# Linear attention of a decoder layer: part of the feature-map work moved from VectorE to GpSimd, and the key sums moved to the end of a tile

## What is computed

```python
def _feature_map(t, K):
    f = jnp.einsum('hdf,bhld->bhlf', K, t)
    feats = jnp.concatenate([jax.nn.softmax(f, axis=-1), jax.nn.softmax(-f, axis=-1)], axis=-1)
    return jnp.maximum(feats, EPS)
q = _heads(x @ Wq); k = _heads(x @ Wk); v = _heads(x @ Wv)
qf = _feature_map(q, Kq)
kf = _feature_map(k, Kk)
kv = jnp.cumsum(kf[:, :, :, None, :] * v[..., None], axis=2)
o = jnp.einsum('bhlf,bhldf->bhld', qf, kv)
z = jnp.einsum('bhlf,bhlf->bhl', qf, jnp.cumsum(kf, axis=2)) + EPS
```

## Time and profile before

| | |
|---|---|
| median of 3 runs | 1230.46 us (1229.52 to 1231.06) |
| the profiled execution | 1229.25 us, span in the trace 1227.0 us |
| mean granted TensorE clock | 0.982 |
| PE busy (share of the span) | 1117.3 us (91%) |
| DVE busy | 962.1 us (78%) |
| ACT busy | 611.1 us (50%) |
| POOL busy | 377.3 us (31%) |

### The profile page before, as it was taken

The page is one execution under the profiler, slowest core; times in us unless marked ns, Lnnn a source line. Parts: engine busy times, 40 slices in busy tenths (PEclk is TensorE's granted clock), DMA queues, the critical chain, the costliest instruction groups (busy, mean ns, idle before and its releaser), DMA issues. The chain is left out here.

```text
span 1227.0 us, 30062 instructions
## 1 busy us (share of the span) xinstructions
PE 1117.3 (91%) x11860; PEld 719.6 (59%) x11861; DVE 962.1 (78%) x1769; ACT 611.1 (50%) x1166; POOL 377.3 (31%) x355
## 2 busy tenths in 40 slices
PE   6698898899899999879999999999999957999996
PEld 5577777777788878643443344334444334666765
DVE  6889978987888788888788677877889556777757
ACT  4233343334333433227777677776788822444443
POOL 4432245222522222113201320222110414656651
PEclk9899999999999999999999999999999988999998
DMA  7100001000400000524720570065050144221225
GB/s 240 41 8 1 2 28 53 2 1 1 80 2 2 1 1 2 81 59 81 152 34 8 114 146 2 9 127 108 2 211 3 53 80 145 65 64 60 63 62 205
DMA packets 60045, 73.65 MB, mean 60 GB/s; under 512 B 14404, under 2 KB 51140, under 8 KB 59188
## 3 DMA queue, kind: packets, MB, share of 16 engines
q1 hardware_dynamic: 56132, 61.56, 21.0%
q0 software_dynamic: 3792, 10.36, 2.7%
HBM read 52.86 MB, written 18.78 MB: 58 GB/s over the span
## 5 line engine op out<-in xcount | busy, mean ns | idle before, releaser
L1791 DVE TENSOR_REDUCE neg_max<-pS 128x1 f32<-128x1024 f32 x238 | 284.9, 1220 | 56.2 <-PE pS L1574 56.0
L1706 ACT ACTIVATE pt<-pR 128x512 f32<-128x512 f32 x512 | 286.5, 600 | 80.1 <-PE pR L1597 75.3
L1597 PE MATMUL pR<-qs,ks 100*32 100x512 bf16 x2048 | 191.2, 383 | 3.1 <-ACT pt L1706 1.6
L1574 PE MATMUL pS<-ks,qs 100*32 100x512 bf16 x1904 | 145.9, 381 | 5.1 <-issue 1.9
L1611 PE MATMUL b_pO<-pt,b_v 128*32 128x512 f32 x1024 | 135.9, 605 | 2.9 <-ACT pt L1706 2.3
L1597 PEld LDWEIGHTS pR<-qs,ks 100*32 100x32 bf16 x2048 | 56.2, 96 | 95.3 <-issue 25.6
L324 POOL TENSOR_TENSOR kf<-kf,fsum 128x2048 f32<-128x2048 f32 (+1 forms) x17 | 58.2, 3422 | 163.8 <-DVE fsum L933 163.8
L324 POOL TENSOR_TENSOR qs<-qs,fsum 128x2048 f32<-128x2048 f32 (+1 forms) x17 | 58.5, 3446 | 142.7 <-DVE fsum L933 142.7
L1453 POOL COPY qs<-max_rows 3x512 bf16<-3x512 bf16 x60 | 36.6, 610 | 209.3 <-ACT max_rows L1699 206.3
L745 ACT COPY qfT<-pT 128x512 f32<-128x512 f32 x64 | 37.3, 582 | 122.7 <-PE pT L466 122.7
L1574 PEld LDWEIGHTS pS<-ks,qs 100*32 100x32 bf16 x1904 | 51.4, 97 | 74.3 <-issue 35.7
(11 more groups left out here) (376 smaller groups left out, 2270.8 us busy)
## 6 DMA issues: line engine op xcount, KB each, us to landing
qs<-q_scr SPq DMA_DIRECT2D x24, 256.0 KB
ks<-k_scr SPq DMA_DIRECT2D x7, 768.0 KB
k_scr<-f SPq DMA_DIRECT2D x18, 256.0 KB, 2.8
ks<-in_L_ffn_w_dram SPq DMA_DIRECT2D x2, 2048.0 KB, 11.1
ks<-in_L_ffn_w_dram SPq DMA_DIRECT2D x4, 1024.0 KB, 8.5
ks<-y_rows SPq DMA_DIRECT2D x16, 256.0 KB, 5.1
ks<-k_scr SPq DMA_DIRECT2D x6, 512.0 KB
cx<-in_ctx_dram SPq DMA_DIRECT2D x3, 768.0 KB, 12.3
```

Source lines behind the costliest of these rows:

```text
L1574: ins = pe.matmul(pS1[q:q + XV, slot, 512 * half:512 * half + 512], qs[0:KR, bass.ds(par, 1), h, P * t + q:P * t + q + XV].rearrange("r a ...
L1597: ins = pe.matmul(ring[bank][q:q + XV, :], ks[0:KR, bass.ds(par, 1), h, P * j + q:P * j + q + XV].rearrange("r a n -> r (a n)"), qs[0:KR, ...
L1706: nc.scalar.activation(pt[:, j % 2, i, :], ring[bank], ACT.Exp).then_inc(exp_done, 1)
L1791: nc.vector.tensor_reduce(neg_max[:, hg % 2, u // G, u % G:u % G + 1], pS1[:, u % 2, :], AX_X, ALU.max, negate=True).then_inc(max_done, 1)
```

## The change

The diff, with what the steps need:

```diff
+        low_less_high = sb("low_less_high", [P, 2, H])
+        drained = [sem("k_drained"), sem("q_drained")]
+        POOL_FROM = (2, 1)
+        def bank_drained(eng, m, t, half_of):
+            if t < POOL_FROM[m]:
+                eng.wait_ge(shifted[m], 2 * t + half_of + 1)
+            else:
+                eng.wait_ge(drained[m], 2 * (t - POOL_FROM[m]) + half_of + 1)
 # GpSimd
+                def clamp(m, t, par, hs=slice(0, H), part=1):
+                    pool.wait_ge(scaled[m], scaled_after(m, t, part))
+                    nc.gpsimd.tensor_scalar(feat[m][:, par, hs], feat[m][:, par, hs], FEAT_EPS, None,
+                                            ALU.max).then_inc(f_ready[m], 1)
+                def other_side(m, t, half_of, par):
+                    pool.wait_ge(drained[m], 2 * (t - POOL_FROM[m]) + half_of + 1)
+                    hs = slice(8 * half_of, 8 * half_of + 8)
+                    nc.gpsimd.tensor_tensor(feat[m][:, par, hs, HD:F2],
+                                            low_less_high[:, m, hs].unsqueeze(2).broadcast_to([P, H // 2, HD]),
+                                            feat[m][:, par, hs, 0:HD], ALU.subtract).then_inc(shifted[m], 1)
-                        if not (last and c == TB - 1):
-                            scale(1, TB * b + c + 1, (c + 1) % 2)
+                        if has1:
+                            other_side(1, t + 1, 0, 1 - par)
+                            clamp(0, t + 1, 1 - par)
+                            other_side(1, t + 1, 1, 1 - par)
+                            for half_of, hs in enumerate(HALVES):
+                                scale(1, t + 1, 1 - par, hs, half_of)
+                                clamp(1, t + 1, 1 - par, hs, half_of)
                         if (b, c) == (0, TB - 1):
                             split_k(0)
                             split_k(1)
-                        if not (last and c >= TB - 2):
-                            scale(0, TB * b + c + 2, c % 2)
+                        if has2:
+                            other_side(0, t + 2, 0, par)
+                            other_side(0, t + 2, 1, par)
+                            scale(0, t + 2, par)
                         if (b, c) == (0, TB - 1):
                             split_k(2)
                             split_k(3)
 # TensorE: project_q and project_v wait by bank_drained; query transposes wait for their half of the clamps
-                    wait(pe, shifted[0], 2 * t + half + 1)
+                    bank_drained(pe, 0, t, half)
+                        if m == 1 and g % 2 == 0:
+                            pe.wait_ge(f_ready[m], 2 * t + g // 2 + 1)
 # VectorE
+                    if t >= POOL_FROM[m]:
+                        nc.vector.tensor_tensor(low_less_high[:, m, hs], lo[:, m, hs], hi[:, m, hs], ALU.subtract)
+                    ins = nc.vector.tensor_tensor(feat[m][:, par, hs, 0:HD], f, ..., ALU.subtract)
+                    if t >= POOL_FROM[m]:
+                        ins.then_inc(drained[m], 1)
+                        return
-                            if g == 1 and has1:
-                                clamp(0, t + 1, 1 - par)
-                            if g == G - 1 and has1:
-                                clamp(1, t + 1, 1 - par)
-                            denominators(0, t + 2, par, own)
                         if final:
                             turned_maxima()
@@
                         x1_statistics(t)
+                        if has2:
+                            denominators(0, t + 2, par, own)
```

More of the change, by code:

```diff
@@ L320, in scale @@
                 def scale(m, t, par, hs=slice(0, H), part=1):
-                    wait(pool, summed[m], t + part + 1)
+                    wait(pool, summed[m], t + part + 1 if t == 0 else t + 2)
                     e = feat[m][:, par, hs].rearrange("p h (s f) -> p (h s) f", s=2)
@@ L325, in scale, with scaled_after @@
                                             ALU.mult).then_inc(scaled[m], 1)
+                def scaled_after(m, t, part):
+                    if m == 1:
+                        return 2 * t + part + 1
+                    return t + part + 1 if t == 0 else t + 2
+                def clamp(m, t, par, hs=slice(0, H), part=1):
[8 more added lines that the diff above has]
+                                            feat[m][:, par, hs, 0:HD], ALU.subtract).then_inc(shifted[m], 1)
                 power(2, TB, T)
@@ L377, in batch @@
                                                     ).then_inc(x1_norm, 1)
-                        if not (last and c == TB - 1):
-                            scale(1, TB * b + c + 1, (c + 1) % 2)
+                        t, par = TB * b + c, c % 2
+                        has1, has2 = not (last and c == TB - 1), not (last and c >= TB - 2)
+                        if has1:
[5 more added lines that the diff above has]
+                                clamp(1, t + 1, 1 - par, hs, half_of)
                         if (b, c) == (0, TB - 1):
@@ L448, in project_q @@
                 def project_q(t, half, par):
-                    wait(pe, shifted[0], 2 * t + half + 1)
+                    bank_drained(pe, 0, t, half)
                     project(1, half, par, proj[1])
                 def project_v(t, half, par):
-                    wait(pe, shifted[1], 2 * t + half + 1)
+                    bank_drained(pe, 1, t, half)
                     project(2, half, par, v_proj)
@@ L458, in transposes @@
                     for m in (1, 0):
-                        if t == 0 and g % 2 == 0:
-                            wait(pe, f_ready[m], g // 2 + 1)
+                        if m == 1 and g % 2 == 0:
+                            pe.wait_ge(f_ready[m], 2 * t + g // 2 + 1)
+                        elif t == 0 and g % 2 == 0:
+                            pe.wait_ge(f_ready[m], g // 2 + 1)
                         elif g == 0:
-                            wait(pe, f_ready[m], t + 2)
+                            pe.wait_ge(f_ready[m], t + 2)
+                        if g == 0:
                             wait(pe, oT_ready, 2 * t)
@@ L918, in shift @@
                     own.wait()
-                    nc.vector.tensor_tensor(feat[m][:, par, hs, 0:HD], f,
-                                            hi[:, m, hs].unsqueeze(2).broadcast_to([P, H // 2, HD]), ALU.subtract)
+                    if t >= POOL_FROM[m]:
+                        nc.vector.tensor_tensor(low_less_high[:, m, hs], lo[:, m, hs], hi[:, m, hs], ALU.subtract)
+                    ins = nc.vector.tensor_tensor(feat[m][:, par, hs, 0:HD], f,
+                                                  hi[:, m, hs].unsqueeze(2).broadcast_to([P, H // 2, HD]),
+                                                  ALU.subtract)
+                    if t >= POOL_FROM[m]:
+                        ins.then_inc(drained[m], 1)
+                        return
                     nc.vector.tensor_tensor(feat[m][:, par, hs, HD:F2],
@@ L927, in denominators @@
                     if t:
-                        wait(dve, scaled[m], t + 1)
+                        wait(dve, scaled[m], 2 * t if m == 1 else t + 1)
                     d = fsum[:, m, 2 * hs.start:2 * hs.stop]
```

## The result

| | before | after |
|---|---|---|
| median | 1229.99 us (4 runs) | 1333.22 us (4 runs) |
| range | 1229.06 to 1231.06 | 1325.98 to 1334.80 |
| profiled span | 1227.0 us | 1332.3 us |
| POOL busy | 377.3 us | 600.8 us |
| mean granted TensorE clock | 0.982 | 0.939 |

The changed kernel is slower by 8.3%: ratio 1.083, 95% interval 1.079 to 1.087. The forecast was 1264 us, in a range of 1236 to 1290: the sign was right, the size was three times too small.

What follows compares the result with a forecast made beforehand. PE was taken as the bound, DVE close behind. Per-tile terms summed to +34.3 us: 1263.6 us against the profiled 1229.25, 1264.8 against the median 1230.46. Forecast 1264 us, range 1236 to 1290 at 8 in 10.

Steps and rivals of the forecast that it cites:

- The clamp's price: POOL's clamp, priced by the cast of 1024 elements: 1.05 us for a half, 1.9 us for the whole.
- the prediction's own sign of being wrong: Listed signs: subtractions of 0.2 us throughout, a POOL clamp other than 1.9 us, or PE without waits in tiles 4 and 8.
- The upper bound in the sum: POOL's clamp at most at the scale's own rate: 1.91 us for a half, 3.62 us for the whole.
- The held difference: DVE's first 128x8 subtraction in a plain tile, held by POOL's key scale until 8.45: 1.9 us lost.
- frame 16.1: DVE's query sums in a plain tile, counted from the start of chunk_scores(t, 0): 16.1 against 14.72, +1.4 us.
- One race: DVE's normalise in a plain tile, due at 10.3, to run at 10.5, ahead of POOL's key clamp at 10.95.
- dear clamp: Rival: POOL's clamp at the scale's rate, second difference held 1.7 us longer in some 13 tiles, +22, 1286 us; chance 0.15.
- The rival by proportion: POOL's clamp by the TENSOR_SCALAR row in proportion: POOL full, over 29 us a tile, kernel above 1330 us; chance 0.05.
- Tiles 4 and 8: Negative sides, ACT's exponentials and copies queue behind the splits: +7.8 us in tile 4, +7.5 in tile 8, 15.3 together.
- No hold: Rival: the 128x8 differences slip between POOL's instructions or are too small to be held; +9, 1239 us; chance 0.17.
- faster: Rival: DVE's load bounds every tile, its 4 us end PE's waits except x_rest; net -5.5, 1225 us; chance 0.10.
- The `x_rest` wait: PE's 0.92 us wait at project_k, behind update(3), stays with any lighter DVE: floor of about 10 us over 11 times.

Runs made afterwards that it cites:

- e1: The changed kernel with GpSimd's clamp replaced by an in-place copy, so nothing is clamped there: 1264.8 us, ratio 1.028.
- e2: The changed kernel with GpSimd's clamp replaced by the subtraction of a broadcast zero column, so nothing is clamped there: 1297.9 us, ratio 1.053.
- e8: The changed kernel with 40 unused transposes on TensorE ahead of chunk_scores(t, 3) in nine tiles: 1327.7 us, ratio 1.077.
- e6: The changed kernel with clamps back on VectorE and query scale whole, plus the six splits spread over GpSimd's list: 1244.8 us, ratio 1.010.
- e5: The changed kernel with clamps back on VectorE and query scale whole, plus the small differences made by GpSimd: 1245.6 us, ratio 1.010.
- e7: The edits of e5 and e6 together, with clamps on VectorE and negative sides on GpSimd: 1227.3 us, ratio 0.994.
- e12: e7 with x_rest put ahead of the update of g = 3: 1219.3 us, ratio 0.990.
- e10: The kernel before with key sums at the end of the tile and x_rest(t+2) ahead of update(3): 1216.4 us, ratio 0.986.
- e4: The changed kernel with both sides of the shift on VectorE and only the clamps on GpSimd: 1268.0 us, ratio 1.032.

## Why the prediction was wrong

- **The clamp's price was the step that failed.** "Nearest in form and size is the cast" gave 1.9 us for 2048 elements; it measured 5.36. The estimate of about 1.8 us that stood beside it, from one-input work going roughly at line rate, failed with it. A clamp other than 1.9 us was also the prediction's own sign of being wrong. The upper bound in the sum, the scale's rate (3.62 us), was no bound. The one row of the same instruction kind was there, 0.70 us for 128 elements, and I set it aside as mostly fixed cost. By the two clamp sizes the rate is (5364 - 2767) / 1024 = 2.5 ns per element and about 0.2 us fixed: neither "mostly fixed" nor the 11 us of proportion. e1 shows that this term carries the net miss of the time: 1264.8 us with the assumed price, 68.4 less than with the real one. It acts in two ways, by the hold of `normalise` (5.60 us in five tiles) and by the second negative side queued behind the clamp (tiles 9 and 13).
- **The sum of the other terms held, partly by luck.** The held difference was to be 1.9 us long and was 1.95. The negative side was to take 1.05 us and took 1.04. Query sums in e1's tile 6 came 16.2 us after `residual` (279.53 - 263.31), worked out as frame 16.1 - 0.15 = 15.95. The plain tiles grew by 1.7 us each (1.4), tile 8 by 7.8 (7.5), tile 5 by 5.6 (5.0). But tile 4 grew by 10.5 us (7.8), tiles 1 and 2 together fell by 1.1 us (3.0), tiles 7 and 11 together fell by 1.1 (worked out to rise by 1.8), tiles 9 and 13 rose by 1.8 each (3.0), tile 3 by 1.3 (2.4) and tile 14 by 2.0 (1.0). These misses cancel; that e1 meets the forecast within a microsecond is more than its parts earn.
- **One race was called wrongly.** I had let `normalise` slip in ahead of the key clamp. In tile 6 it was held by it, 5.60 us in the changed kernel and 2.11 in e1. In tiles 3, 7 and 11 it did slip in (0.61 us); in 7 and 11 the clamp then held the second difference instead (2.29 us in tile 7). In e1's tile 6 the lost race made no difference to the sum, since the second small difference was then no longer held (0.17 us).
- **The "dear clamp" rival named the place and not the weight.** e2, at the scale's rate, took 1297.9 us against 1286. The rival by proportion had "above 1330" and 0.05 of the chance; that time came out, and by luck. Its condition, a full GpSimd at 29 us a tile, wasn't met (22.4 of 36.3 us in tile 6) and the clamp cost half of what it assumed (5.4 us, not 11). It counted only GpSimd's work, and neither the hold of 5.6 us nor the clock.
- **The clock was missing from the sum.** From the query sums to the next tile's start it was 14.55 us and is 327.07 - 310.66 = 16.4 us in tile 6 after. e8 gives 1.8 us per plain tile back. How much of the 68 us it is in all isn't settled.
- **Tiles 4 and 8** were right in mechanism: ACT behind a negative side behind the splits, and e6 takes it away. With the clamp's real price they went from 40.0 and 37.3 us (e1) to 48.8 and 44.4.
- **"No hold" and "faster" fell.** e5, with the held differences gone from VectorE, is 16 us faster. e7 and e12 show what the faster rival would need, and that DVE's lighter load is worth 0.4 us in a plain tile (27.6 us in e12, 28.0 in e10).
- The `x_rest` wait was called a floor "with any lighter DVE". It is one for the load and not for the order: with 2.4 us per tile less on VectorE it was still 13.2 us (e7), and e10 takes most of it.

## What to carry to other kernels

Before work is moved to GpSimd, price its instruction by a row of the same kind, and where there is none keep the range open upwards; a cast or a tensor_tensor is no bound for a tensor_scalar. Then look for each VectorE instruction that will meet it, with two SBUF inputs or SBUF to SBUF by tensor_scalar: it can cost what is left of GpSimd's running instruction, or the whole of the next one, not its own length, and it holds up everything behind it. Look as well at what is queued behind the new instruction on GpSimd itself. Before moving work at all, see whether the waits of the bound engine come from load or from order: two swaps of order were worth 1.4% here, and the negative sides taken off VectorE (2.4 us per tile) nothing in the whole.

## What the runs showed of the hardware

- GpSimd's tensor_scalar maximum on float32 takes 2.5 ns per element (5.36 us for 128x2048). The in-place copy takes 0.83 (1.91 us for 2048, 1.06 for 1024), the tensor_tensor with a broadcast operand 1.7. VectorE needs 1.22 us for the same clamp.
- A VectorE subtraction of 128x8 with both inputs in SBUF was held up to 3.3 us by GpSimd (0.17 us alone), a tensor_scalar of 128x256 up to 5.6 us (0.40 alone).
- The two are let go at different moments. Beside a scale or a copy the subtraction ended with GpSimd's instruction. Beside the clamp it ended 1.7 us before it, in all five cases of the changed kernel, while `normalise` ended 0.15 us behind it. Twelve key differences that fell into a half clamp (2.77 us) 0.9 us or more after its start weren't held at all (0.17 us). Tile 7, POOL's timeline and then DVE's (the subtraction ends at 340.94, the clamp at 342.64):

```profile
337.24 5.40 POOL L345 TENSOR_SCALAR kf<-kf 128x2048 f32<-128x2048 f32 x1
...
338.65 2.29 DVE L961 TENSOR_TENSOR low_less_high<-lo,hi 128x8 f32<-128x8 f32 x1
```

- Near a change of GpSimd's instructions a VectorE instruction can lose its place. `normalise` starts in the record at 300.81, 0.13 us before the negative side ended, and the key clamp recorded from 300.91 ran before it. In tile 7 it starts 0.47 us before that end (336.80, 337.27) and went in first. In e4, with GpSimd idle, `normalise` starts at 298.90 and the clamp at 298.98, and it was held all the same, 5.58 us. A recorded start is thus no proof of who asked first. The Trainium skill (SBUF — State Buffer, section Who interferes with whom) says that whoever issues first gets the ports for the whole instruction; these rows of `normalise` fit that if VectorE asks a little after its recorded start, which no run here shows.
- After a wait of 4.6 us within an otherwise full stretch TensorE's granted clock fell to 1.2 GHz for 6.8 us. With the wait filled by unused transposes it stayed at 2.4 GHz.
